# Splitting the first layer's weights, making its rotary tables and clearing its shifted inputs inside the last steps of the recurrence

## The reference

```python
# 1. conditioned recurrence, state h of 16 x 256 per sequence, 32 steps
def step(h, inputs):
    ad, bd, xt, ct = inputs
    h = jnp.clip(h * ad[:, :, None] + bd[:, :, None] * xt[:, None, :], -10.0, 10.0)
    yt = jnp.einsum('bd,bdh->bh', ct, h)
    return (h, yt)
y = ys.transpose(1, 0, 2) + D * xn
return y * jax.nn.silu(gate) @ W_out.T

# 2. six layers of local attention (16 heads of 64, window 32) and gated FFN
for i in range(DEPTH):
    x = attn_layer(shift_tokens(x), Wqkv[i], q_scale[i], k_scale[i], Wo[i]) + x
    x = ffn_layer(shift_tokens(x), ln_g[i], ln_b[i], W1[i], b1[i], W2[i], b2[i]) + x
```

## Time and profile before

| quantity | value |
|---|---|
| median of 3 runs | 2817.21 us (2816.74 to 2818.28) |
| the profiled execution's own time | 2818.77 us |
| span of its instructions | 2817.0 us |
| PE busy | 2682.6 us (95%) |
| DVE busy | 2594.5 us (92%) |
| ACT busy | 2248.4 us (80%) |
| POOL busy | 2112.0 us (75%) |
| last instruction of the first block ends | 376.26 us |
| first instruction of the second block | 376.53 us |
| first projection of the second block | 381.46 us |

### The profile page before, as it was taken

How to read it: one execution, slowest core, us unless ns; L and a number is a source line. 1 busy time by engine, 2 the same in 40 slices (tenths; PEclk the granted TensorE clock), 3 DMA queues, 4 the chain that set the end, 5 groups by cost and what they waited for, 6 DMA issues and landing times.

```text
span 2817.0 us, 92972 instructions
## 1 busy us (share of the span) xinstructions
PE 2682.6 (95%) x36469; PEld 2057.4 (73%) x36469; DVE 2594.5 (92%) x3384; ACT 2248.4 (80%) x3786; POOL 2112.0 (75%) x1530
## 2 busy tenths in 40 slices
PE   8999978999999999999999999999999999999998
PEld 7677756777777777777777777777777777777776
DVE  7999968999999999999999999999999999989996
ACT  5899957878788787878878788787878878778786
POOL 5866658777777778778778787778787787777773
PEclk9999999999999999999999999999999999999999
DMA  1000013232223322223232332322233322222223
GB/s 59 24 2 2 2 39 76 72 73 68 71 65 76 74 71 67 70 70 74 70 73 66 74 72 68 80 63 68 66 74 73 73 66 68 67 67 67 58 65 102
DMA packets 103735, 178.41 MB, mean 63 GB/s; under 512 B 29366, under 2 KB 52724, under 8 KB 103412
## 3 DMA queue, kind: packets, MB, share of 16 engines
q1 hardware_dynamic: 102388, 174.60, 25.5%
q10 hardware_dynamic: 1152, 1.20, 0.1%
HBM read 22.62 MB, written 2.10 MB: 9 GB/s over the span
## 4 chain that ended last, share of the span: by engine, by line
PE 32%; POOL 15%; issue 15%; ACT 10%; DMA 8%; DVE 4%; SPq 1%; POOLq 0%; ACTq 0%; DVEq 0%
PE pa L942 10%; POOL spare L1700 8%; DMA kT<-spare 7%; PE px L971 6%; PE ps L1002 3%; PE pg L1084 3%; PE pg L1060 3%; PE px L1016 3%; PE pg L1075 3%; ACT spare L1267 2%; POOL xs_lo L1686 2%; DVE ss L1482 2%; POOL pr L1738 2%; POOL spare L1709 1%; ACT spare L1213 1%
## 5 line engine op out<-in xcount | busy, mean ns | idle before, releaser
L1700 POOL TENSOR_TENSOR spare<-spare,qk_t 128x1024 f32<-128x1024 f32 x384 | 911.2, 2394 | 11.4 <-POOL xs_lo L1686 8.1
L942 PE MATMUL pa<-w_hi,xs_hi 128*128 128x512 f32 x1152 | 510.0, 443 | 27.2 <-DVE qk_t L1498 9.3
L1716 POOL TENSOR_TENSOR sm<-sm,inv 128x512 f32<-128x512 f32 x192 | 202.0, 1052 | 434.6 <-DVE sm L1520 365.4
L1498 DVE TENSOR_TENSOR qk_t<-pa,rot 128x1024 f32<-128x1024 f32 x384 | 465.2, 1212 | 5.0 <-ACT spare L1220 4.2
L1489 DVE TENSOR_TENSOR spare<-pa,rot 128x1024 f32<-128x1024 f32 x384 | 465.2, 1211 | 0.0
L1482 DVE TENSOR_REDUCE ss<-spare 128x16 f32<-128x1024 f32 x384 | 458.2, 1193 | 6.2 <-ACT spare L1213 5.4
L942 PE MATMUL pa<-w_hi,xs_lo 128*128 128x512 f32 x1152 | 458.2, 398 | 0.3 <-DMA pT<-prT 0.3
L942 PE MATMUL pa<-w_lo,xs_hi 128*128 128x512 f32 x1152 | 454.2, 394 | 0.0
L971 PE MATMUL px<-ident_sb,spare 128*128 128x128 f32 x3072 | 408.5, 276 | 18.5 <-POOL spare L1709 10.0
L1709 POOL TENSOR_TENSOR spare<-spare,inv 128x1024 f32<-128x1024 f32 x192 | 366.0, 1906 | 69.8 <-ACT inv L1252 66.4
L971 PEld LDWEIGHTS px<-ident_sb,spare 128*128 128x128 f32 x3072 | 341.6, 141 | 104.7 <-issue 46.5
(11 more groups left out here) (211 smaller groups left out, 5921.4 us busy)
## 6 DMA issues: line engine op xcount, KB each, us to landing
kT<-spare SPq DMA_DIRECT2D x384, 256.0 KB, 3.7
pT<-prT SPq DMA_DIRECT2D x768, 64.0 KB, 2.0
w_part<-in_Wqkv SPq DMA_DIRECT2D x40, 192.0 KB, 3.7
wo<-in_Wo SPq DMA_DIRECT2D x6, 512.0 KB, 5.5
c_h<-in_x SPq DMA_DIRECT2D x4, 512.0 KB, 9.2
wo<-in_W SPq DMA_DIRECT2D x6, 341.0 KB, 4.7
spare<-in_Wqkv SPq DMA_DIRECT2D x1, 1536.0 KB, 6.7
spare<-in_x SPq DMA_DIRECT2D x4, 256.0 KB, 4.0
```

The costliest lines, as they stand in the source:

```text
L942: last = pe.matmul(pa[(u + c) % 2][:, half * 512:half * 512 + 512], x[:, j * P:(j + 1) * P], w[:, at], start=(k == 0), stop=(k == 2))
L1498: dve.tensor_tensor(halves(qk_t[:, c, :]), halves(pa[(3 * j + c) % 2][:])[:, :, ::-1, :], table.unsqueeze(1).to_broadcast([P, HEADS, 2, DH ...
L1700: pool.tensor_tensor(qk_r[:, c, :], qk_r[:, c, :], qk_t[:, c, :], ALU.add)\
```

## The change

Fifteen operations move from the second block into the first (four of ACT, three of DVE, eight of POOL), and three memsets move from POOL to DVE.

- ACT casts the three pieces of `w_hi` and loads the activation table in its loop turn t = 32 (`t == S`), behind `copy_zT(30)`. `write_res(30)`, `copy_zT(31)` and `write_res(31)` stand behind them.
- DVE subtracts the three pieces of `w_lo` in its turn t = 32, ahead of `gated(31)`; each waits for ACT's cast.
- POOL clears `xs_hi` and `xs_lo` and makes the first rotary tables behind its last `side(31)`, once ACT has made all outer products.
- `kT`, `pT` and `fs` are cleared by DVE at the start of the second block, not by POOL.
- For that `w_hi[0]`, `w_lo[0]`, `xs_hi`, `xs_lo` and `rot` live across both blocks. `w_lo` and the others are allocated over the place of `xn`, whose values the first block still reads up to the last outer product; `qk_t` and `gt` go there too. `w_hi` has a place of its own.

```diff
@@ cond_block, ACT @@
                     write_res(t - 3)
                     copy_zT(t - 2)
+                    if t == S:
+                        act.wait_ge(w0_loaded, 16)
+                        for c in range(3):
+                            at = slice(c * INNER, (c + 1) * INNER)
+                            act.copy(first["w_hi"][:, at], room[:, at]).then_inc(first["w0_hi"], 1)
+                        act.preload_act_table_set(EXP_LN)
@@ cond_block, POOL, behind its loop @@
+                pool.wait_ge(s["u_ready"], NPAIR * (S - 1))
+                pool.wait_ge(s["xnT_done"], S)
+                pool.memset(first["xs_hi"][:].bitcast(F32), 0.0).then_inc(first["xs_zeroed"], 1)
+                pool.memset(first["xs_lo"][:].bitcast(F32), 0.0).then_inc(first["xs_zeroed"], 1)
+                pool.wait_ge(first_loaded, 3 * 16)
+                rotary_tables(pool, 0, first["rot"], rot_const, qk_scale, first["rot_ready"])
@@ cond_block, DVE @@
                     clip(t)
+                    if t == S:
+                        for c in range(3):
+                            at = slice(c * INNER, (c + 1) * INNER)
+                            dve.wait_ge(first["w0_hi"], c + 1)
+                            dve.tensor_tensor(first["w_lo"][:, at], room[:, at], first["w_hi"][:, at].bitcast(F32),
+                                              ALU.subtract).then_inc(first["w0_ready"], 1)
                     gated(t - 1)
@@ stack, ACT @@
-                act.preload_act_table_set(EXP_LN)
                 act.wait_ge(s["xs_zeroed"], 2)
                 shift_hi(0, 0, 0, True)
-                act.wait_ge(w0_loaded, 16)
-                for c in range(3):
-                    at = slice(c * INNER, (c + 1) * INNER)
-                    act.copy(w_hi[0][:, at], w_raw[:, at]).then_inc(s["w0_hi"], 1)
-                    if c == 0:
-                        shift_hi(0, 0, 1, True)
+                shift_hi(0, 0, 1, True)
@@ stack, DVE @@
-                for c in range(3):
-                    at = slice(c * INNER, (c + 1) * INNER)
-                    dve.wait_ge(s["w0_hi"], c + 1)
-                    dve.tensor_tensor(w_lo[0][:, at], w_raw[:, at], w_hi[0][:, at].bitcast(F32), ALU.subtract)\
-                        .then_inc(s["w0_ready"], 1)
+                dve.memset(kT[:], 0.0).then_inc(s["zeroed"], 1)
+                dve.memset(pT[:], 0.0).then_inc(s["zeroed"], 1)
+                dve.memset(fs[:], 0.0).then_inc(s["zeroed"], 1)
@@ stack, POOL @@
-                pool.memset(xs_hi[:].bitcast(F32), 0.0).then_inc(s["xs_zeroed"], 1)
-                pool.memset(xs_lo[:].bitcast(F32), 0.0).then_inc(s["xs_zeroed"], 1)
                 pool.wait_ge(s["xs_zeroed"], 2)
                 shift_lo(0, 0, 0, True)
                 shift_lo(0, 0, 1, True)
-                pool.wait_ge(first_loaded, 3 * 16)
-                rotary_tables(0)
-                pool.memset(kT[:], 0.0).then_inc(s["zeroed"], 1)
-                pool.memset(pT[:], 0.0).then_inc(s["zeroed"], 1)
-                pool.memset(fs[:], 0.0).then_inc(s["zeroed"], 1)
                 pool.wait_ge(s["zeroed"], 7)
@@ build @@
+        first = {"w_hi": ctx.enter_context(nc.sbuf_tensor("first_w_hi", [DM, 3 * INNER], F32R))}
+        with nc.sbuf_tensor("c_xn", [P, S, DI], F32) as xn:
+            pass
+        first.update((name, ctx.enter_context(nc.sbuf_tensor(f"first_{name}", shape, dt))) for name, shape, dt in (
...
```

More of the change, by code:

```diff
@@ L58, in wait_for, with rotary_tables, cond_block @@
     eng.wait_ge(sem, count)
-def cond_block(nc, d, res, spare, w0_loaded, ident, rot_const, qk_scale, first_loaded):
+def rotary_tables(pool, l, rot, rot_const, qk_scale, rot_ready):
+    for c in range(2):
+        sc = qk_scale[:, c, :]
+        pool.tensor_tensor(rot[:, l % 2, 2 * c, :], rot_const[:, 2 * c, :], sc, ALU.mult).then_inc(rot_ready, 1)
+        for f in range(2):
+            to, frm = slice(f * DH // 2, (f + 1) * DH // 2), slice((1 - f) * DH // 2, (2 - f) * DH // 2)
+            pool.tensor_tensor(rot[:, l % 2, 2 * c + 1, to], rot_const[:, 2 * c + 1, to], sc[:, frm], ALU.mult)\
+                .then_inc(rot_ready, 1)
+def cond_block(nc, d, res, spare, w0_loaded, ident, rot_const, qk_scale, first_loaded, first, xn):
     with ExitStack() as ctx:
@@ L639, in _, with stack @@
                     clip(t)
+                    if t == S:
[4 more added lines that the diff above has]
+                                              ALU.subtract).then_inc(first["w0_ready"], 1)
                     gated(t - 1)
-def stack(nc, d, res, spare, w0_loaded, ident, rot_const, qk_scale, first_loaded):
+def stack(nc, d, res, spare, w0_loaded, ident, rot_const, qk_scale, first_loaded, first):
     with ExitStack() as ctx:
@@ L660, in stack @@
         floor_c = sb("floor_c", [P, 2])
-        w_hi = [sb(f"w_hi{k}", [DM, 3 * INNER], F32R) for k in range(2)]
-        w_lo = [sb(f"w_lo{k}", [DM, 3 * INNER], F32R) for k in range(2)]
-        w_raw = spare[:, 0:3 * INNER]
+        w_hi = [first["w_hi"], sb("w_hi1", [DM, 3 * INNER], F32R)]
+        w_lo = [first["w_lo"], sb("w_lo1", [DM, 3 * INNER], F32R)]
         w_part = sb("w_part", [DM, W_PART])
@@ L679, in stack @@
         ln_par = sb("ln_par", [DM, 3])
-        rot = sb("rot", [P, 2, 4, DH])
-        xs_hi = sb("xs_hi", [DM, GTOK], F32R)
-        xs_lo = sb("xs_lo", [DM, GTOK], F32R)
+        rot, xs_hi, xs_lo, qk_t, gt = (first[name] for name in ("rot", "xs_hi", "xs_lo", "qk_t", "gt"))
         sq = spare[:, (GT + 2) * INNER:(GT + 3) * INNER]
@@ L724, in stack @@
         s = {n: sem(n) for n in names}
+        s.update((n, first[n]) for n in ("w0_hi", "w0_ready", "xs_zeroed", "rot_ready"))
         heads = lambda ap: ap.rearrange("p (h e) -> p h e", e=DH)
@@ L1808, in build @@
         first_loaded = ctx.enter_context(nc.semaphore("first_loaded"))
-        cond_block(nc, d, res, spare, w0_loaded, ident, rot_const, qk_scale, first_loaded)
-        stack(nc, d, res, spare, w0_loaded, ident, rot_const, qk_scale, first_loaded)
+        first = {"w_hi": ctx.enter_context(nc.sbuf_tensor("first_w_hi", [DM, 3 * INNER], F32R))}
+        with nc.sbuf_tensor("c_xn", [P, S, DI], F32) as xn:
+            pass
+        first.update((name, ctx.enter_context(nc.sbuf_tensor(f"first_{name}", shape, dt))) for name, shape, dt in (
+            ("w_lo", [DM, 3 * INNER], F32R), ("xs_hi", [DM, GTOK], F32R), ("xs_lo", [DM, GTOK], F32R),
+            ("rot", [P, 2, 4, DH], F32), ("qk_t", [P, 2, INNER], F32), ("gt", [P, 3, GTOK], F32)))
+        first.update((name, ctx.enter_context(nc.semaphore(name))) for name in ("w0_hi", "w0_ready", "xs_zeroed", "rot_ready"))
+        cond_block(nc, d, res, spare, w0_loaded, ident, rot_const, qk_scale, first_loaded, first, xn)
+        stack(nc, d, res, spare, w0_loaded, ident, rot_const, qk_scale, first_loaded, first)
 _INS = {
```

20 lines of the change are left out of this document (4 added, 16 removed).

## The result

The changed kernel took **2824.87 us** (median of 9 runs, 2822.83 to 2825.99), the kernel before 2816.74 (median of 9 runs beside them, 2813.89 to 2819.60). The ratio is 1.0028 with a 95% interval of 1.0020 to 1.0036: 5.6 to 10.1 us slower, where 1.9 were forecast. The profiled execution took 2823.92 us for a span of 2822.1. Its first block runs about 1.2 us late from the start (a load landed later) and 1.3 us late at the last clip, so I compare distances, not absolute times.

The account below looks back on a forecast made before the run. PE (95%) and DVE (92%) were taken as close to full, but only the chain at the border of the blocks was priced: 4.46 + 0.2 - 2.80 = +1.9 us, so 2819.1 us, with an 8-in-10 range of 2816.4 to 2821.6.

Parts of the forecast that it names:

- Step 1, the delay of `gated(31)`: End of first block: casts and subtractions queued ahead of `gated(31)` delay the transposes and the border by +4.46 us.
- that rival: DVE's subtractions before `gated(31)` keep their old pace, 1.56 + 3.02 us, for a reason other than POOL: 2820.2 us; chance 0.08.
- Step 2, the last clip: End of first block: POOL's new memsets may hold up DVE's last clip, on the chain; +0.2 us, bounds 0 and 0.34.
- Step 3, the second block: Start of second block: less work there, so PE starts at B + 2.76 and the sum of squares comes 2.80 us earlier.
- B: The first instruction of the second block, at 376.53 in the kernel before; the forecast counts times from it.
- the slow rival: Start of second block: DVE's memsets hold off POOL's first `xs_lo` half, 2.8 us late: +4.7, 2821.9 us; chance 0.10.
- Rival of the full clock: First v and q matmuls, second block: at PE's full clock their 5.44 us halve, -2.7; total 2816.4 us; chance 0.20.
- Step 4, the addresses: Whole kernel: SP's list is the same and other buffer addresses move no instruction; costed at nothing.
- the sign of it: Border and sum of squares as forecast but time over 3 us off: layers react to start or buffer places; step 4 failed.
- The second half of the same step: Behind the border: everything is tied to B, so what is left at the sum of squares goes through to the end.

Follow-up runs that it names:

- Experiment 2: Changed kernel with ACT's casts and table load moved ahead of `write_res(t - 3)` and `copy_zT(t - 2)`, into ACT's idle stretch: 2819.13 us, ratio 1.0006.
- Experiment 3: Changed placement, and of the changed order only POOL's memsets and tables at the end of the first block: 2821.76 us, ratio 1.0018.
- 11: All buffers at 32, casts in the idle stretch, plus 12 and 12 small PE matmuls ahead of q and v of tile 0: 2817.34 us, ratio 1.0000.
- 12: Kernel before plus 20 and 14 small PE matmuls ahead of q and v of tile 0: 2822.04 us, ratio 1.0013.
- experiment 1: Kernel before in its own order, with its buffers where the change puts them: 2821.08 us, ratio 1.0016.
- experiment 9: Changed kernel in its own order, padded so weights and shifted inputs all lie at 32 modulo 64: 2822.63 us, ratio 1.0017.
- 6: Changed kernel with casts in the idle stretch, and odd layers' weights some 25 KB further up, still at 32 modulo 64: 2820.90 us, ratio 1.0009.
- 10: Kernel before in its own order, with 32 bytes of padding ahead of the shifted inputs, putting them at 0 modulo 64: 2825.08 us, ratio 1.0026.
- experiment 8: Changed kernel with casts in the idle stretch, padded so weights and shifted inputs all lie at 32 modulo 64: 2817.68 us, ratio 0.9998.
- 7: Changed kernel with casts in the idle stretch, and shifted inputs padded to 32 modulo 64, even weights at 0, odd at 32: 2819.27 us, ratio 1.0004.
- 5: Changed kernel with casts in the idle stretch, and odd layers' weights padded to 0 modulo 64: 2817.96 us, ratio 1.0000.
- experiment 4: The changed kernel again, unaltered, beside the other runs for a second profile: 2824.30 us, ratio 1.0024.

## Why the prediction was wrong

*Step 1, the delay of `gated(31)`: right in mechanism, 0.6 us short.* The three subtractions took 3.50 us (forecast 3.49), not the old 1.56 and 3.02, and POOL was idle beside them; that rival is out. Step 1 was to move the border by 4.46 and it moved by 5.08. Up to the transposes it was 4.26. The other 0.82 is the drain behind them: after 4.10 us of waiting PE ran at the lower level, as one window of the changed kernel shows, and the transposes took 0.69 instead of 0.38 and the projection 1.22 instead of 0.71 us.

```profile
380.00:383.00 3.00, 1.91 (x6) 1.22 (x6) 0.03 (x1) 0.74 (x2) 0.00 (x0) 0.50 0.00 0
```

I had moved these instructions later without asking which clock they would meet there. Experiment 2 takes the whole delay away by two lines.

*Step 2, the last clip: right.* +0.2 us forecast; clip and matmuls measured 0.19 longer from start to start. Here the rule of the Trainium skill, "SBUF — State Buffer", section "Who interferes with whom", is seen: POOL's product of 64 columns, issued into the clip, lasted until the clip's end. For the memset the trace agrees only in part: it reached 0.33 us into the clip, and the clip took 0.19 longer. Experiment 3 shows no more than that from POOL.

*Step 3, the second block: right.* PE started at B + 2.69 (forecast 2.76), the sum of squares at B + 6.78 (6.77). DVE's memsets took 3.38 us and did not hold POOL: `xs_lo` started at B + 1.20 and took 2.95 for all four, so the slow rival is out. The same section says that a DVE instruction with at most one SBUF input, outside the two-port modes, does not contend with GpSimd; for the memset, which reads nothing, this row agrees.

*Rival of the full clock: partly.* The v/q group got back 0.7 us of 2.7 in the changed kernel; its clock was 0.70 over 393.40 to 398.70, against 0.51. The price was too high all the same: at 1.00, in experiments 11 and 12, the group gained no more than these 0.7.

*Step 4, the addresses: this is the step that failed.* "Other buffers lie at other addresses, which moves no instruction; I cost it at nothing." No instruction moved, and it cost about 2.7 us by the group periods (2.2 of them clear), +2.0 to +7.0 us by the total of experiment 1. Some two thirds of it go with the 32 bytes between weights and shifted inputs. The prediction had named the sign of it (border and sum of squares about right, and the time more than 3 us off), but no term and no chance. The second half of the same step, "Everything behind B is tied to B, so what is left at the sum of squares goes through to the end", failed too: the second group took 2.3 us more in both profiles of the changed kernel and 2.0 in experiment 9, but 0.04 in experiment 1. That this is PE's clock is read from how the two go together, not from a run that changes the clock alone: with no time at the lower level in that group it took 0.0 to 0.3 us more (1, 3, 6, 10, 11), with 3.4 us 0.7 (2), with 6.8 us 1.2 and 1.4 (8, 7), with 10.2 us 1.9 to 2.3 (5, 9, 4 and the changed kernel). Only 12 falls out, with 6.8 us and nothing lost.

The sum as measured: 2.5 at the sum of squares, -0.7 in the v/q group, +2.3 in the second group, +2.7 by placement, in all 6.8 us, within the interval of 5.6 to 10.1. The changed kernel's first profile alone shows less, 3.8 us from the last clip on, and its second one (experiment 4) 9.0. What stays open:
- Why PE's clock falls in the second group under the changed order. It repeats there in three profiles of three, but the kernel before also has idle stretches of PE there and keeps its clock. Experiments 2 and 5 to 8 share one other order, and there the same group took 0.7, 1.9, 0.0, 1.4 and 1.2 us more than before.
- 2.0, 2.6 and 3.2 us in experiments 1, 3 and 6, which measured more than their profiles' parts add up to; in 6 the parts lie outside the interval. Single profiles carry differences of 1 to 2.5 us at the borders of layers in either direction, and the intervals are 5 us wide, so I don't read a cause into it.
- What in the 64 bytes is slow: which operand and which access. No run separates the two further, and only 0 and 32 were tried. With all at 0 in odd layers the matmuls follow each other as with all at 32, and yet the group kept 0.056 us.

None of the twelve is measurably faster than the kernel before. The one that keeps the change's idea and loses nothing measurable has the casts in the idle stretch and all buffers at 32 (experiment 8).

## What to carry to other kernels

When a change redeclares or shares buffers, compare their addresses modulo 64 before and after, above all of operands that meet in a dense run of matmuls; a few bytes of padding are a cheap control experiment that moves no instruction. Work put into "idle" time goes where the queue stands, not where the gap is: place it ahead of the instruction that waits, and price what is moved later at the clock that it will meet. A saving of 2 to 5 us at one border can be half gone 100 us later, with PE's clock as a part of it, so follow the offset between the two traces to the end before calling it a gain.

## What the runs showed of the hardware

- The period of a group of tiles (49.4 us at full clock) grew by 0.07 to 0.14 us when the weights and the inputs of the same matmuls lay 32 bytes apart modulo 64. From start to start of a matmul of 128x512 this is about 2 ns of 230. In odd layers of the changed kernel the distance went from 230.5 to 233.6 ns with another part on top (53 pairs a group, so 0.16 us, of which 0.09 reached the period). I had expected that the address doesn't matter.
- A POOL product of 128x64, 0.32 us long alone (367.24 in the changed kernel), lasted 2.36 us when it met DVE's clip of 128x4096, and the clip, which met a POOL memset, 2.48 instead of 2.29.
- DVE's memset of 128x2048 took 1.76 us beside POOL's subtractions, and those took 2.95 for four of 64x256, no longer than alone (two in 1.44).
- PE at the lower level: two transposes 0.69 instead of 0.38 us, four matmuls of 128x128 1.22 instead of 0.71.
